# Regrouped low halves, first expert pair and last norms, and a new order of a decoder body, in a fused decoder, cross-attention and expert kernel

## The reference

```python
# x: (16, 256, 256) f32, ctx: (16, 120, 192) f32
x = layernorm(x + decoder(x))      # 4 layers, pre-norm: causal attention with alibi, 16 heads of 16,
                                   #   then 256 -> 1024 (gelu) -> 256
x = layernorm(x + cross(x, ctx))   # attention over ctx, then 256 -> 512 (relu) -> 256
x = layernorm(x + ffn(x))          # 8 experts, the 2 best of a router per token:
    logits = xf @ Wr + br;  weights = softmax(top 2 of logits, others -inf)
    h   = gelu(einsum('td,edh->eth', xf, W1) + b1)
    out = einsum('etd,te->td', einsum('eth,ehd->etd', h, W2) + b2, weights)
```

## Time and profile before

| | |
|---|---|
| median of three runs | 3588.39 us (3587.18 to 3588.78) |
| the profiled execution | 3585.7 us, its span 3584.1 us |
| granted TensorE clock, mean | 0.973 of full |
| busy: PE, DVE, ACT, POOL | 93%, 74%, 65%, 42% of the span |
| decoder, cross, experts end at about | 1923.8, 2268, 3584.1 us |
| DMA | 124.54 MB, mean 35 GB/s |

### The profile page before, as it was taken

One profiled execution on the slowest core, in us unless ns is written; L12 is line 12 of the kernel. 1 busy time (PEld: TensorE's weight loads), 2 busy tenths in 40 slices (PEclk: granted clock), 3 DMA queues, 4 the chain that ended last, 5 costly groups with the idle time before them and its releaser, 6 DMA issues. The chain is left out here.

```text
span 3584.1 us, 90173 instructions
## 1 busy us (share of the span) xinstructions
PE 3325.9 (93%) x36704; PEld 2316.1 (65%) x36704; DVE 2662.9 (74%) x5168; ACT 2344.8 (65%) x3525; POOL 1505.6 (42%) x1356
## 2 busy tenths in 40 slices
PE   5899999999999999999994888699999999999997
PEld 3667676676767666676762555466666666666665
DVE  4766667676676767667635897798888888888888
ACT  4677777767677776767762675566666665666654
POOL 1343333434333343433334552354454444445443
PEclk8999999999999999999996999799999999999999
DMA  3100111101111011100102212100000000000001
GB/s 120 42 28 29 40 49 36 38 29 40 40 45 33 24 37 52 45 29 29 35 5 75 66 63 74 51 24 26 1 26 26 1 26 1 26 1 26 1 13 36
DMA packets 102762, 124.54 MB, mean 35 GB/s; under 512 B 17648, under 2 KB 90608, under 8 KB 100080
## 3 DMA queue, kind: packets, MB, share of 16 engines
q1 hardware_dynamic: 102352, 118.78, 10.0%
HBM read 50.13 MB, written 8.39 MB: 16 GB/s over the span
## 5 line engine op out<-in xcount | busy, mean ns | idle before, releaser
L2582 POOL TENSOR_TENSOR e_hT<-e_h,e_hT 128x512 f16<-128x512 f32 x512 | 615.0, 1203 | 648.0 <-ACT e_hT L2348 625.3
L2342 ACT ACTIVATE e_h<-e_h,e_b 128x512 f32<-128x512 f32 x512 | 365.4, 714 | 436.6 <-DVE e_h L2434 436.6
L984 DVE TENSOR_REDUCE mx<-maxima_pair 128x4 f16<-128x1024 f32 (+1 forms) x384 | 470.2, 1225 | 239.7 <-PE maxima_pair L483 237.2
L75 PE MATMUL bank<-xT,w_half 128*128 128x512 f16 x2304 | 533.0, 382 | 3.9 <-DVE xT L927 3.9
L790 ACT ACTIVATE PR<-scores_pair 128x1024 f32<-128x1024 f32 x384 | 392.5, 1022 | 126.1 <-PE scores_pair L500 117.8
L1087 POOL TENSOR_TENSOR QK<-qk,QK 128x512 f16<-128x512 f32 x128 | 148.3, 1159 | 629.9 <-ACT qk L722 433.3
L1094 POOL TENSOR_TENSOR hT<-h,hT 128x512 f16<-128x512 f32 x256 | 296.4, 1159 | 260.3 <-ACT hT L777 222.3
L2280 PE MATMUL bank<-VS,e_hT 128*128 128x256 f16 x3072 | 389.0, 273 | 9.5 <-DVE VS L2393 5.7
L2280 PE MATMUL bank<-e_w,e_hT 128*128 128x256 f16 x3072 | 390.3, 274 | 1.2 <-POOL e_hT L2582 1.0
L2280 PEld LDWEIGHTS bank<-VS,e_hT 128*128 128x128 f16 x3072 | 299.9, 98 | 117.3 <-POOL e_hT L2582 7.1
L75 PEld LDWEIGHTS bank<-xT,w_half 128*128 128x128 f16 x2304 | 215.9, 98 | 244.4 <-issue 9.5
(11 more groups left out here) (199 smaller groups left out, 6867.1 us busy)
## 6 DMA issues: line engine op xcount, KB each, us to landing
QS<-QK SPq DMA_DIRECT2D x240, 128.0 KB, 2.1
KS<-QK SPq DMA_DIRECT2D x192, 128.0 KB, 2.1
PR<-in_expert_weights SPq DMA_DIRECT2D x16, 1024.0 KB, 4.9
w_raw<-in_weights SPq DMA_DIRECT2D x48, 256.0 KB, 3.6
c_x<-in_x SPq DMA_DIRECT2D x8, 512.0 KB, 4.0
xT_f<-c_xT SPq DMA_DIRECT2D x8, 512.0 KB, 3.7
stage<-xT_f SPq DMA_DIRECT2D x4, 1024.0 KB, 5.8
out<-stage SPq DMA_DIRECT2D x8, 512.0 KB, 3.1
```

The lines of the kernel that those rows point to most:

```text
L75: last = pe.matmul(out, stat(a, k), mov(b, k), start=(k == 0 and n == 0), stop=(k == tiles - 1 and n == 2))
L984: dve.tensor_reduce(out, src, AX.X, ALU.max, negate=True).then_inc(mx_in.sem, 1)
L2342: act.activation(h32[r % 2][:, j, :], h32[r % 2][:, j, :], ACT.Gelu, bias=b1[:, e, m:m + 1], scale=1.0 / WS)\
L2582: pool.tensor_tensor(hT[r % 2][1][:, f, part], h32[r % 2][:, j, :], hT[r % 2][0][:, f, part], ALU.subtract)\
```

## The change

**Decoder, PE order of a steady body.** V values, KS key scores, RS row scores, OS turned outputs, OT turn, T1 and T2 turned norms, QK queries and keys, AT attend, OP attended, MT turned maxima, H hidden, Y shrunk; a + marks the next group.

Before: KS00 RS20 V0 OS0 OS1 KS01 OS2 OS3 RS21 V1 OT0 T1-0 KS02 RS22 OT1 Y0 RS30 KS10 T1-1 OP0 MT2 AT0 KS11 RS31 OP1 QK0 QK1 KS12 RS32 QK2 Y1 KS20 MT3 AT1 KS21 Y2 T2-0 +RS00 KS22 T2-1 QK3 KS30 +RS01 Y3 KS31 +RS02 AT2 KS32 +RS10 H0 H1 +RS11 H2 H3 +RS12 +MT0 H4 H5 H6 H7 +MT1 AT3

After: V0 KS00 RS20 OS0 OS1 V1 RS21 KS01 OS2 T1-0 T1-1 RS22 KS02 OS3 Y0 MT2 RS30 OT0 OT1 KS10 QK0 QK1 RS31 KS11 AT0 OP0 RS32 KS12 OP1 KS20 MT3 AT1 QK2 KS21 Y1 +RS00 KS22 T2-0 QK3 +RS01 KS30 Y2 T2-1 +RS02 KS31 Y3 +RS10 KS32 +MT0 AT2 +RS11 H0 H1 H2 +RS12 H3 H4 H5 H6 H7 +MT1 AT3

ACT's order follows it (values 0 first; norm1's full and high halves before exps(0,2) and behind it; exps(1,1) and (1,2) together; qkv's and f1's conversions behind values 1). SP sends `maximum(n + 1, 0)` ahead of `heads_high(n + 1, 1)`.

**Decoder, DVE and POOL.** `hidden_low` 4 to 7 go from POOL to the end of DVE's body, behind norm1 of group n+2; POOL's `add_row(g, 1)` goes to the end of its body.

```diff
             if back:
                 outputs(kind, n, 0)
                 outputs(kind, n, 1)
+            if front:
+                maxima(n, 2, 1)
+            if back:
                 outputs(kind, n, 2)
+            if front:
+                maxima(n, 2, 2)
+            if swap == 3:
+                weights(l, "f1")
+            if back:
                 outputs(kind, n, 3)
             if swap == 1:
                 weights(l, "qkv")
-            if front:
-                maxima(n, 2, 1)
+            if ahead:
+                low(0, n + 1, 0, xh1, xf1, xl1)
+                low(0, n + 1, 1, xh1, xf1, xl1)
...
                     norm1(n + 2, group(g, 2))
+            if back:
+                for m in range(KF // 2, KF):
+                    hidden_low(n, m)
```

```diff
                 add_row(group(g, -1), 2, xb2)
+                hidden_low(n, 0)
+                hidden_low(n, 1)
+            if ahead:
+                query_key_low(n + 1, 3)
+            if back:
+                hidden_low(n, 2)
+                hidden_low(n, 3)
             if front:
                 if swap == 2:
                     pool.wait_ge(row_in[1].sem, row_in[1].after(l))
                 pool.wait_ge(z1.sem, z1.after(n))
                 add_row(g, 1, xb1)
-            if ahead:
-                query_key_low(n + 1, 3)
-            if back:
-                hidden_low(n, 0)
-                hidden_low(n, 1)
-                hidden_low(n, 2)
-                hidden_low(n, 3)
-                hidden_low(n, 4)
-                hidden_low(n, 5)
-                hidden_low(n, 6)
```

**Cross.** In the last bodies (n = NG, NG + 1, NG + 2) ACT also makes the high halves of the first pair (7 operations), of the first expert's other four weight blocks and of its second weights in one operation of 128x2048; DVE makes the four sums outside the router's chain and one more low half; POOL makes the first pair's 4 sums and 7 low halves in n = NG + 2:

```diff
+                for p in (3, 1, 2):
+                    first_pair_low(p)
+                first_pair_sum(6)
+                first_pair_sum(4)
+                for p in (5, 7, 6, 4):
+                    first_pair_low(p)
```

```diff
+        def bias(pair, u):
...
+            pool.tensor_tensor(scaled[:, :], b2[(E - 1) % 2][:, 0, :], weight[:, at:at + 1].to_broadcast([P, D]), ALU.mult)\
+                .then_inc(bias_last.sem, 1)
+            wait(pool, bias_last, pair, 2 * u + 1)
+            pool.tensor_tensor(x[:, n, :], x[:, n, :], scaled[:, :], ALU.add).then_inc(bias_last.sem, 1)
...
                 if i == 2:
                     norm_of(pair - 1)
+                if i == 3:
+                    for tile in range(TT, PT):
+                        scale(pair - 1, tile)
```

More of the change, by code:

```diff
@@ L577, in body @@
             if front:
+                values(kind, n, 1)
+                row_scores(n, 2, 1)
                 key_scores(n, 0, 1)
@@ L619, in body @@
             if front:
-                key_scores(n, 1, 2)
[L621 to L625, removed]
+                row_scores(n, 3, 1)
+                key_scores(n, 1, 1)
+                attend(n, 0)
+            if back:
+                if swap == 3:
+                    part_ready("o", l)
+                attended(kind, n, 0)
+            if front:
+                row_scores(n, 3, 2)
+                key_scores(n, 1, 2)
+            if back:
+                attended(kind, n, 1)
             if front:
@@ L1004, in body @@
                 outputs(kind, n, 1)
-                outputs(kind, n, 2)
-                outputs(kind, n, 3)
-            if swap == 1:
-                weights(l, "qkv")
             if front:
@@ L1011, in body @@
             if back:
-                outputs_low(kind, n, 0)
+                outputs(kind, n, 2)
             if front:
@@ L1016, in body @@
                 weights(l, "f1")
+            if back:
+                outputs(kind, n, 3)
+            if swap == 1:
+                weights(l, "qkv")
             if ahead:
                 low(0, n + 1, 0, xh1, xf1, xl1)
+                low(0, n + 1, 1, xh1, xf1, xl1)
+            if tail:
+                shrunk(kind, n, group(g, -2), 0)
+            if back:
+                outputs_low(kind, n, 0)
+            if front:
+                maxima(n, 3, 0)
             if back:
                 outputs_low(kind, n, 1)
-            if tail:
-                shrunk(kind, n, group(g, -2), 0)
-            if front:
-                maxima(n, 3, 0)
-            if ahead:
-                low(0, n + 1, 1, xh1, xf1, xl1)
-            if back:
-                attended(kind, n, group(g, -1), 0)
-                attended(kind, n, group(g, -1), 1)
             if front:
@@ L1032, in body @@
             if back:
-                norm2_stats(n, group(g, -1))
+                attended(kind, n, group(g, -1), 0)
             if front:
@@ L1036, in body @@
             if back:
+                attended(kind, n, group(g, -1), 1)
+                norm2_stats(n, group(g, -1))
                 norm2_root(n, group(g, -1))
```

541 lines of the change are left out of this document (307 added, 234 removed).

## The result

The changed kernel takes 3642.50 us (median of four runs, 3634.63 to 3645.71) against 3588.22 for the kernel before (four runs, 3587.18 to 3588.78): 1.0148 times as long, 95% interval 1.0131 to 1.0166. It is slower by 54 us, where 12 us less were forecast. The profiled execution took 3642.49 us at a span of 3640.7, 56.6 more than the span of before.

What follows compares the result with a forecast made beforehand. PE is busy nearly throughout, so only its gaps count, in the steady decoder set by DVE's order. Decoder +11.5, late stages -9, -3.5, -10 and -0.9 sum to -11.9: 3573.8 profiled, 3576.5 us median, range 3548 to 3602.

Steps and rivals of the forecast that it cites:

- The forecast case: Whole kernel: plain bodies at 56.6 us from a longer DVE chain, other stages gaining; 3576.5 us in all, chance 0.50.
- the corrections (-0.75 and +1.0): Plain body's stall of 1.6: less for cheaper add_row hits, more for add_row behind the lows and values(0) meeting a hidden_low.
- Rival B: DVE's chain between row_scores(1,2) and row_scores(2,1) hit throughout: stall 2.8, plain body 57.6, total 3599 us; chance 0.20.
- Swap 1: Three decoder bodies converting qkv: maxima (2,1) and (2,2) move ahead of the conversions, 61.08 to 57.7 us, -10 in all.
- Swap 3: Three decoder bodies converting f1 and f2: gap grows from 5.49 to about 7, 60.72 to 62.2 us, +4.5 in all.
- Start and end: Decoder's first and last bodies: no tail covers the new order at the start, last bodies lose the 1.07; +1.
- From cross to experts: Sums, prologue and second weights' low halves move into the last cross bodies, less slow clock, less slip: -9.
- First expert: Rounds 4 to 13: half the x_low go to POOL and the sums no longer wait; -3.5.
- Last expert: Three rounds with a norm: bias to POOL, scales to the next round, half on ACT; three times -3.4, -10.
- Behind the last matmul: After the last matmul the eight scales are split over two engines, less one small operation: -0.9.
- Rival A: Plain bodies: the chain fits and PE doesn't stall, -25 there; total 3535 us, or 3556 with half the stall; chance 0.12.
- Rival C: Late stages give back half: norm rounds stay at 14 us, cross bodies slip by 3; total 3588 us; chance 0.18.

Runs made afterwards that it cites:

- e2: Changed kernel with POOL's add_row(g,1) back at its old place, ahead of the lows; hidden_low 4 to 7 stay on DVE: 3552.97 us, 0.9889.
- e5: e2 with f2's low halves on DVE moved from ahead of maxima (1,0) to behind maxima (1,1): 3527.59 us, 0.9820.
- e6: e4 with one part of the decoder's change: hidden_low 4 to 7 at the end of DVE's body instead of on POOL: 3540.57 us, 0.9859.
- e4: Changed kernel with the decoder's orders and tile list as in the kernel before; cross and experts as changed: 3570.95 us, 0.9944.
- e1: Changed kernel with hidden_low 4 to 7 back on POOL, ahead of the late add_row(g,1): 3744.0 us, 1.0417.
- e8: e2 with x_low 1, 2 and 5 of the later pairs back on DVE, one execution: rounds 4 to 13 take 107.1 us.
- e7: e2 with all eight lows on POOL (new PE order, add_row(g,1) at its old place): 3639.47 us, 1.0127.
- e3: Changed kernel with norm1 of group n+2 put ahead of maxima (1,2) on DVE: 3682.06 us, 1.0249.

## Why the prediction was wrong

Between the forecast for the profiled execution and its measured span lie 68.5 us (+56.6 for -11.9). The plain bodies, swap 2 among them, are 30 of these, swap 3 is 12, swap 1 is 9, the decoder's start and end are 8.5, and so are the late stages.

*The forecast case* had the right place and mechanism for the plain body, and the terms of that body's sum held up but for one: the hits. "I take 1.6 + 0.2: the corrections (-0.75 and +1.0) nearly cancel" is the step that failed. Hits of 3.9 us had been assumed for the 1.6, and 4.8 were measured: cheaper hits there were, but more of them, so that the -0.75 was not there at all. I had reasoned that four `add_row` operations of 0.69 hit for less than lows of 1.16 and kept the number of hits of the old trace (four); but with POOL's operations on end each tiny operation meets the next POOL operation, so six were hit (two by 0.95, four by 0.48, together 3.8) and the scales by 1.0. The text's own upper bound, 2.6 us of stall, is what was measured (2.62). With 0.3 more of small gaps and busy time the plain body came to 57.75 where 56.6 was forecast, 1.15 too long, which is 26 us over 23 bodies. The evidence stood in the earlier trace rows: POOL's pauses, not its busy time, let DVE pass one to three operations in the kernel before. The new place of `add_row(g,1)` was counted at nothing for its reader, and that held; what it costs the chain is 2.98 us (e2).

*The clock* had no term in the plain body. At a gap of 2.6 us five of the twenty plain bodies ran at 0.97 and took 58.9, some 6 us in all; the twenty plain bodies are 58.1 on average (1713.4 less 552.0 for the nine swap bodies), +2.15 each, so +43, and swap 2's three another +3.2, where +16 was forecast for all of them. *Rival B* had a body of 57.6 and a run of 3599: its place was right and its stall of 2.8 us nearly so, though six of the twelve were hit and not all; even its sum fell 43 us short, since the clock, swap 1, swap 3, the last bodies and the late stages were mis-sized around it.

*Swap 1* (-10 forecast) gave -0.9: the old gap went, as e2's 56.4 shows, and the new stall of 2.6 with its clock (0.97, 1.5 us a body) took its place. *Swap 3* (+4.5) gave +16.5: the f2 conversions held `row_scores(1,1)` for 3.7 us and the clock fell to 0.92; forecast as a gap of 7 (it was 7.1), the price of the clock left out (PE busy 59.36 instead of 55.23). e5 shows the cause of that wait. *Start and end* (+1) gave +9.5; e6 ends its decoder with the old order in 48.5, 33.5 and 42.3 us where e2 takes 49.9, 37.6 and 44.1, so the new order costs 7.3 of the 8.2 us in the last three bodies; that it lacks its front work there is my reading and was not tried.

*From cross to experts* (-9) gave -6.8: cross slipped by 3.3 (2.4 forecast), and the wait for the second weights' low halves fell from 5.67 to 4.1 only: the four take 5.37 us (from 2356.65) where they took 3.03 before. In the trace three of POOL's lows stand beside them, from 2356.99 and in 4.48 us; before, POOL's three (3.70) ended 0.7 us into DVE's four. So the two held each other up, as in the decoder; no run tried it. PE's timeline answers to the earlier trace rows:

```profile
2346.20 1.01 PE L2371 MATMUL maxima_pair<-spare,QS 128*128 128x512 f16 x2 [3.35 <-PEq L2147]
...
2362.07 1.46 PE L2393 MATMUL bank<-VS,e_hT 128*128 128x256 f16 x6 [4.13 <-DVE VS L2498]
```

*First expert* (-3.5) gave +1.2. At the full clock (e4) the same rounds, 2 to 15, take 1.4 us less than before, so the sum was too high by 2; the other 2.6 are the clock of 0.98 there and the gaps that come with it. *Last expert* (-10) gave -9.9, but partly by luck: the rounds up to the last gave -12.1, since PE's gaps there fell from 12.0 to 2.9 us and the slow clock went (a round with a norm takes 9.98 us, where 11.5 was forecast), and the last round gave 2.2 back. There PE waits 2.5 us for POOL's low halves (0.2 before); ACT's four scales (2.06 us) stand ahead of three of that round's gelus, which I take for the cause and no run tried. *Behind the last matmul* (-0.9) gave +0.5: the last scale ends 0.4 us sooner, and from there to the end, which is the output's transfer, it is 4.66 us for 3.76; why was not tried.

*Rival A* (no stall, for the chain fits) was not what this kernel does, but it is what e2 is, one call away. *Rival C*'s sum for the late stages (11.9) lies nearer to the measured 14.9 than my 23.4 does. Its slip of the cross bodies by 3 us came true (3.3); its norm rounds of 14 us did not (9.98).

The sentence that weighed the Trainium skill, page "SBUF — State Buffer", section "Who interferes with whom", holds in the plain bodies read above: tiny operations with inputs in SBUF wait for POOL's operation beside them, a TENSOR_REDUCE out of PSUM stays at 1.21 to 1.23 us under any POOL load. The prediction quoted it for two SBUF inputs; here the operations of L132, L135, L138 and L160, with one tensor for input, wait just the same. The page says that it holds the other way round as well, and here POOL's `values` takes 1.85 to 1.99 instead of 1.28 where it meets DVE's four lows (e2, and the changed kernel at 746.72).

## What to carry to other kernels

A chain of tiny dependent DVE operations beside POOL doesn't slow down by POOL's busy share: in these runs it advanced by one operation for each POOL operation as long as those stood on end, so twelve operations of 0.2 us took 12 us (e1). Before moving work to or on POOL, look which tiny chain runs at that time, and count POOL's operations on end there, not its load; a few cheap operations moved right behind others can cost more than the large ones that were moved away to make room. And price a PE gap of 2 to 3 us with the clock behind it: here that added 1.2 us to a gap of 2.6 in a quarter of the bodies. Compare stretches of two kernels only where the trace grants both the same clock (e8).

## What the runs showed of the hardware that I had not expected

The lockstep itself: six tiny operations (128x4) at a pitch of 1.13 us beside six POOL operations in 6.79 us (e1), four at 0.69 beside POOL's at 0.70, and 0.20 when POOL is idle. A DVE operation of 256 elements per partition waits as well (the scales, 2.38 us instead of 1.38 beside one `values`). Two limits: it takes operations that stand on end (with three POOL lows in 3.71 us, in the changed kernel's last norm, tiny operations pass in between and six of thirteen are hit, for 3.2 us), and BATCH_NORM_STATS2 and BATCH_NORM_AGGREGATE were not hit (1.40 and 0.38 us beside POOL's operations in the changed kernel; 1.39 and 0.38 in e6, where POOL is idle during the second).

The clock: with a gap of 1.07 us per body (before) it stays at its full level in plain bodies; with 2.1 to 2.7 one plain body in two (e7) to four (the changed kernel) takes 1.2 to 1.5 us more at a granted clock of 0.97 (1099.18 to 1158.10, above); with 3.4 to 3.5 (e3) most bodies do, by up to 2.6. The size of the gap alone does not decide it: the smaller gap of e7 lowers the clock in more bodies than the larger one of the changed kernel, and swap 3 of the kernel before has 5.49 us of gap, in four waits, at the full clock. With 5.0 (e1) all take 61.5 to 61.9, of which 56.4 us and more are outside the gaps, 1.4 above the 55.0 of the changed kernel.
